# Image 0 of a deformable convolution: its rows moved in near and far rows by 18 transfers, and its gather indices made in three parts

## The chip, the cores and the metric

The kernel runs on one core of a Trainium2 chip. The metric is the device time in microseconds (us); lower is better. Before the change it is 1011.0 us, the median of 3 runs (1010.9 to 1011.95).

## The reference, cut to what matters

Four layers run one after the other on `x` of shape (2, 32, 64, 64), each on a group-normalised copy of `x` and added to it: an anchor-based normalisation, a graph-like feed-forward layer, a state-space scan over the 4096 pixels of an image, and a deformable 3x3 convolution. The change lies in the last one:

```
offset = _conv(data_im, offset_w)                    # 18 channels: y and x of 9 taps
mask = jax.nn.sigmoid(_conv(data_im, mask_w))        # 9 channels
col = _deform_im2col(data_im, offset, mask)          # bilinear samples at tap + offset, times mask
out = jnp.einsum('op,bphw->bohw', weight, col)
```

For every output pixel and tap the offset convolution says where to sample; the sample is a weighted sum of four corner pixels, all 32 channels of which are read.

## The kernel before, in words

The two images go through the last two layers one behind the other, and they overlap: while the scan of image 1 runs on DVE, ACT and PE, image 0 is already sampled. POOL (GpSimd) fetches the corners. A table in DRAM (`corner_table_0`, `corner_table_1`) holds for every pixel its four corners times 32 channels; one indirect DMA (L780) fetches, for 128 pixels and one tap, 128 rows of it. 128 pixels are a group: group g of an image holds 32 pixels in each of the four quarters of the image, and a quarter is 16 image rows, so that two groups are one image row in each quarter. An image has 32 groups, image 0 with 9 gathers each, image 1 with 6 (the other taps are computed densely). Five slots hold gathered groups. POOL waits at the head of its list for the whole table (`table_in`, L1578) and for the first indices (`idx_ready`, L1579), and before each group for a free slot (`prod_done`, L777); then it issues gather after gather.

`prepare(b)` makes what POOL needs for image b. For image 0 it runs between the scan of image 0 and the projection of image 1. Its steps, engine by engine, in the order in which each engine has them written down:

- DVE: statistics and normalisation (`g4`, L1306), transposition into the table (`tab`, L1311), copies of the right and lower neighbours (L1315 to L1321; L1321 takes what ACT has evicted), then a wait for the image rows (L1326), two memsets of the border columns (L1327, L1328), and after each half of the offset convolution `positions` and `corners` (L1337 to L1348), which write 16 groups of indices; behind them the coefficients, and then the projection of image 1.
- PE: the four shifts for the lower neighbours (L1265), and then, after `g3_ready`, the offset convolution (L1274) in two halves of 512 columns for each of 4 quarters and 3 kernel rows. The trace shows two PE instructions for each matmul of the code.
- ACT: issues three of the six image-row transfers (`load_image`, L1239), and behind them evicts the four shifts (L1288).
- SP (SyncE): issues the other three, then the table in two halves (L1251), each after the copies that it needs, and after the convolution the residuals (L1256).

`G3` holds the normalised image three times, shifted by -1, 0 and +1 pixels, on 96 partitions; `load_image` fills it by DMA from SBUF to SBUF, one transfer for each shift j and each half h of the image, 256 KB each:

```
first = W + h * HALF - (j - 1)
engine.dma_start(G3[32 * j:32 * j + 32, first:first + HALF],
                 g4[64 * b + 32 * h:64 * b + 32 * h + 32, :]).then_inc(l3["g3_in"], 16)
```

Of the kernel before, what the change touches and what calls it, by code (L numbers as in the profile page):

```python
# [20 lines left out]
B, C, H, W = 2, 32, 64, 64  # L21
# [69 lines left out]
def build(nc, x, mats, vecs, wts, bic, anchors, base, sel, out):  # L91
    ctx = ExitStack()
    with ctx:
# [613 lines left out]
        gathered = [sem(f"gathered{k}") for k in range(SLOTS)]  # L707

# [510 lines left out]

        def prepare(b):  # L1220
# [15 lines left out]
            def load_image(engine, h):  # L1236
                for j in range(3):
                    first = W + h * HALF - (j - 1)
                    engine.dma_start(G3[32 * j:32 * j + 32, first:first + HALF],  # L1239
                                     g4[64 * b + 32 * h:64 * b + 32 * h + 32, :]).then_inc(l3["g3_in"], 16)  # L1240

            def sync(sp):
# [3 lines left out]
                load_image(sp, 0)  # L1246
# [6 lines left out]
                sp.wait_ge(l3["off_psum"], 2 * b + 2)  # L1253
# [6 lines left out]
            def tensor(pe, between=nothing):  # L1260
# [8 lines left out]
                pe.wait_ge(l3["g3_ready"], b + 1)  # L1269
                for n in range(2):  # L1270
                    for q in range(4):
                        for dy in range(3):
                            first = q * QUARTER + n * BANK + dy * W
                            last = nc.tensor.matmul(PS[32 * q:32 * q + 32, 4 + n, :], wt[0:96, W_OFF + 32 * dy:W_OFF + 32 * dy + 32],  # L1274
                                                    G3[:, first:first + BANK], start=(dy == 0), stop=(dy == 2))
# [4 lines left out]
            def scalar(act, between=nothing):  # L1280
# [4 lines left out]
                load_image(act, 1)  # L1285
# [10 lines left out]
            def vector(v, between=nothing):  # L1296
# [29 lines left out]
                v.wait_ge(l3["g3_in"], 96 * (b + 1))  # L1326
                vchain(v, nc.vector.memset(cols[0:32, :, 0], 0.0))  # L1327
                tell(v, nc.vector.memset(cols[64:96, :, W - 1], 0.0), l3["g3_ready"], b + 1)  # L1328
# [5 lines left out]
                def positions(half):  # L1334
                    part = slice(16 * half, 16 * half + 16)
                    v.wait_ge(l3["off_psum"], 2 * b + half + 1)
                    vchain(v, nc.vector.transpose(om[:, part, :].rearrange("p g k -> p (g k)"), PS[:, 4 + half, :]))  # L1337
                    vchain(v, nc.vector.tensor_tensor(yx[:, part, :], om[:, part, 0:18], bases[:, part, :], ALU.add))

                def corners(half):  # L1340
                    part = slice(16 * half, 16 * half + 16)
# [6 lines left out]
                    nc.vector.memset(prime[:, 12 + 2 * b + half:13 + 2 * b + half], 0.0).then_inc(l3["idx_ready"], 1)  # L1348

                positions(0)  # L1350
                corners(0)
# [495 lines left out]
```

## Time and profile before

| | |
|---|---|
| median of 3 runs | 1011.0 us |
| the profiled execution's own time | 1014.24 us |
| its span | 1012.0 us |
| mean granted TensorE clock | 0.832 |
| busy: PE, DVE, POOL, ACT | 782.5, 837.1, 580.1, 387.0 us |
| image rows of image 0 issued | from 346.8 us |
| first gather of image 0 | 368.24 us |

Times in the rows are microseconds from the start of the span, durations in microseconds unless ns is said. PE is the matmul engine, PEld its weight load, DVE the VectorE, SPq and ACTq the sequencers of SP and ACT when they issue a DMA. A row of the timeline gives start, duration, engine, line, operation, output<-input, how many are merged in it, and in brackets the idle time before it with what ended it.

### The profile page before, as it was taken

To read this page: it belongs to the slowest core of one execution; us is meant where nothing else is said; L and a number is where in the kernel's file an instruction comes from. 1 tells how busy PE (TensorE), PEld (TensorE's weight loads), DVE (VectorE), ACT (ScalarE), POOL (GpSimd) and SP (SyncE) were. 2 spreads that over 40 slices of the span, in tenths; PEclk is the share of its full clock that TensorE was granted. 3 is DMA by queue.
4 is the path that set the end of the run, shared out by engine and by line. 5 is a ranking of instruction groups with operands and counts; after the bars stand their busy time and mean duration, and the time that the engine had idled before them with its cause. 6 is when DMAs were issued, how large, how long until landed. Compare 5 with 4: busy or idle time off the path is not lost.

```text
span 1012.0 us, 8286 instructions
## 1 busy us (share of the span) xinstructions
PE 782.5 (77%) x2365; PEld 377.3 (37%) x2365; DVE 837.1 (83%) x1161; ACT 387.0 (38%) x544; POOL 580.1 (57%) x528
## 2 busy tenths in 40 slices
PE   2345875677787688676788787869379999999997
PEld 1132322222222124534454444423264444444443
DVE  3889842789999858879998899985989998979884
ACT  1120046854454136311212121101049586776650
POOL 0000000076765037877777777777777777777774
PEclk9666987979999889567777677776559999999998
DMA  5000017000000361111111111128353745444422
GB/s 122 0 0 1 0 31 155 17 0 1 1 1 0 64 133 49 37 52 53 51 50 52 52 49 53 51 64 195 110 139 90 195 136 143 122 123 130 120 65 53
DMA packets 32339, 69.82 MB, mean 69 GB/s; under 512 B 12368, under 2 KB 12624, under 8 KB 31184
## 3 DMA queue, kind: packets, MB, share of 16 engines
q1 hardware_dynamic: 16080, 35.27, 13.2%
q0 software_dynamic: 15360, 31.49, 12.1%
q10 hardware_dynamic: 864, 2.64, 1.2%
q8 instruction: 16, 0.26, 0.1%
q14 instruction: 19, 0.16, 0.0%
HBM read 54.94 MB, written 5.77 MB: 60 GB/s over the span
## 4 chain that ended last, share of the span: by engine, by line
PE 42%; DVE 26%; POOL 7%; issue 6%; ACT 2%; DMA 1%; DVEq 0%; ACTq 0%; POOLq 0%
PE PS L1481 19%; POOL got L780 7%; DVE scratch L1174 6%; PE PS L815 5%; DVE scratch L1100 4%; DVE scratch L1181 3%; PE PS L1057 2%; PE PS L1042 2%; PE PS L1498 2%; DVE prodg L791 2%; PE PS L855 2%; DVE PS L1097 2%; PE PS L1274 2%; DVE prodg L795 1%; PE PS L914 1%
## 5 line engine op out<-in xcount | busy, mean ns | idle before, releaser
L780 POOL DMA_INDIRECT got<-corner_table,idx_slot x405 | 402.8, 995 | 123.4 <-issue 123.4
L1042 PE MATMUL PS<-parts,selb 96*128 96x512 bf16 (+1 forms) x256 | 88.4, 446 | 85.0 <-DVE scratch L1100 45.3
L1057 PE MATMUL PS<-scratch,wt 128*128 128x512 f32 x256 | 146.1, 701 | 0.5 <-DVE scratch L1181 0.5
L1481 PE MATMUL PS<-scratch,UZ 128*128 128x512 f32 (+1 forms) x288 | 133.6, 613 | 2.9 <-DVE scratch L1466 2.9
L780 POOL DMA_INDIRECT got<-corner_table,idx_all x75 | 84.9, 1132 | 60.6 <-DVE prime L1348 38.0
L821 ACT ACTIVATE G<-PS 128x32 f32 (+1 forms) x32 | 6.3, 197 | 250.7 <-PE PS L815 250.6
L815 PE MATMUL PS<-ln_g,w 128*128 128x32 f32 x576 | 101.9, 344 | 0.0
L815 PEld LDWEIGHTS PS<-ln_g,w 128*128 128x128 f32 x576 | 99.3, 268 | 0.0
L1564 POOL MEMSET w<- 128x1152 f32 x1 | 1.1, 1058 | 159.7 <-POOLq L599 159.7
L1042 PEld LDWEIGHTS PS<-parts,selb 96*128 96x128 bf16 x256 | 22.9, 116 | 158.2 <-DVE scratch L1100 59.1
L1458 ACT ACTIVATE scratch<-UZ,knot 128x512 f32<-128x512 f32 (+1 forms) x128 | 81.6, 708 | 0.4
L1481 PEld LDWEIGHTS PS<-scratch,UZ 128*128 128x128 f32 (+1 forms) x288 | 53.2, 193 | 74.9 <-issue 55.8
L1057 PEld LDWEIGHTS PS<-scratch,wt 128*128 128x128 f32 x256 | 58.5, 229 | 57.4 <-issue 47.9
L1100 DVE TENSOR_TENSOR_SCAN scratch<-scratch,carry,PS 128x1024 f32<-128x1024 f32 x32 | 75.1, 2347 | 1.1
L1150 POOL TENSOR_TENSOR scratch<-scratch 128x1024 f32<-128x1024 f32 x16 | 37.6, 2349 | 59.5 <-ACT scratch L1132 59.5
L1481 PE MATMUL PS<-XN,UZ 128*128 128x512 f32 x144 | 65.2, 601 | 0.0
L1139 ACT ACTIVATE PS<-XN,negA 128x1024 f32<-128x1024 f32 x32 | 35.8, 1118 | 60.8 <-DVE scratch L1174 60.8
L1466 DVE SCALAR_TENSOR_TENSOR scratch<-scratch,UZ 128x512 f32<-128x512 f32 (+1 forms) x72 | 45.4, 691 | 4.8 <-ACT UZ L1455 4.5
L1150 POOL TENSOR_TENSOR got<-scratch 128x1024 f32<-128x1024 f32 x16 | 37.6, 2348 | 17.7 <-ACT scratch L1132 17.7
L1466 DVE SCALAR_TENSOR_TENSOR XN<-XN 128x512 f32<-128x512 f32 (+1 forms) x72 | 45.4, 692 | 0.7 <-ACT XN L1455 0.5
L1105 DVE TENSOR_TENSOR scratch<-scratch,PS 128x1024 f32<-128x1024 f32 x32 | 39.1, 1221 | 8.3 <-PE PS L1042 8.2
L1466 DVE SCALAR_TENSOR_TENSOR scratch<-scratch,XN 128x512 f32<-128x512 f32 (+1 forms) x72 | 45.2, 689 | 0.2
(350 smaller groups left out, 1354.8 us busy)
## 6 DMA issues: line engine op xcount, KB each, us to landing
UZ<-dense_rows SPq DMA_DIRECT2D x24, 512.0 KB, 4.1
got<-corner_table,idx_slot POOLq DMA_INDIRECT x405, 2.5
UZ<-dense_rows SPq DMA_DIRECT2D x96, 64.0 KB, 2.2
XN<-ln_g SPq DMA_DIRECT2D x6, 256.0 KB, 5.8
got<-corner_table,idx_all POOLq DMA_INDIRECT x75, 2.5
corner_table<-scratch SPq DMA_DIRECT2D x1, 1056.0 KB, 10.4
corner_table<-XN SPq DMA_DIRECT2D x1, 1056.0 KB, 10.4
X<-in_x SPq DMA_DIRECT2D x4, 256.0 KB
```

What stands on the lines that cost most here:

```text
L780: pool.indirect_dma_start(got[:, slot, tap, :, :].rearrange("p k c -> p (k c)"), None, tables[b], bass.IndirectOffsetOnAxis(ap=index[:, ta ...
L815: last = nc.tensor.matmul(group_psum(slot), w3[:, t, :], colgs[slot][:, t * C:t * C + C], start=False, stop=(t == n - 1))
L1042: last = nc.tensor.matmul(PS[:, first + n, :], selb[:, which, j, :], parts[:, bass.ds(i * CHUNK + n * BANK, BANK)], start=True, stop=True)
L1057: last = nc.tensor.matmul(PS[:, 4 + n, :], wt[:, W_SUM:W_SUM + P], dBC[:, j % 2, n * BANK:(n + 1) * BANK], start=False, stop=(j == PAIRS - 1))
L1100: tell(v, nc.vector.tensor_tensor_scan(hs, dA[:, j % 2, :], banks(0, 2), carry[:, j:j + 1], ALU.mult, ALU.add), sc["h_done"], s + 3)
L1105: nc.vector.tensor_tensor(dBC[:, j % 2, :], hs, banks(2, 2), ALU.mult).then_inc(sc["hc_done"], 1)
L1139: nc.scalar.activation(banks(6, 2), dl[:, c * CHUNK:(c + 1) * CHUNK], ACT.Exp, scale=negA[:, j:j + 1]).then_inc(sc["exp_done"], 1)
L1150: nc.gpsimd.tensor_tensor(dBu[j % 2], dus[c % 2], Bs[j % 2], ALU.mult).then_inc(sc["dbu_done"], 1)
L1174: tell(v, nc.vector.tensor_tensor_scan(hs, banks(6, 2), dBu[j % 2], carry[:, j:j + 1], ALU.mult, ALU.add), sc["h_done"], s + 3)
L1458: nc.scalar.activation(ramps[k][rows, j, :], loads[k][rows, 1, :], ACT.Relu, bias=knot[rows, j:j + 1]).then_inc(de["ramps"], 1)
L1466: nc.vector.scalar_tensor_tensor(ramps[k][rows, j, :], ramps[k][rows, j, :], 1.0, hats[k][rows, :], ALU.min, ALU.mult).then_inc(de["prods" ...
L1481: last = nc.tensor.matmul(PS[:, n % 4, :], steps[rows, j, :, :].rearrange("p b c -> p (b c)"), ramps[k][rows, j, :], start=(j == 0), stop= ...
```

## The change

For image 0 alone each queue moves its image half in near rows (rows 0 to 2 and row 15 of each 16-row quarter, three shifts each, six transfers) and then in far rows (rows 3 to 14, three transfers). Two quarters go in one transfer, as two pieces per partition. That makes 9 transfers on SP and 9 on ACT. Near rows have a semaphore of their own (`g3_near`). DVE clears the border columns of near rows by six memsets and signals `g3_ready`; later it clears those of the far rows by two. The offset convolution and the index arithmetic run in parts of 4, 12 and 16 groups; on DVE `corners(0)` and the far memsets stand before `positions(1)`. POOL waits for the first part's indices before group 0 and for the second's before group 4. Image 1 keeps its six transfers, its two memsets and its two halves.

```diff
+        NEAR_ROWS, FAR_ROWS = ((0, 3), (15, 16)), ((3, 15),)
+            PARTS = ((0, 4), (4, 16), (16, 32)) if b == 0 else ((0, 16), (16, 32))
+            parts_before = 3 * b
-            def load_image(engine, h):
-                for j in range(3):
-                    first = W + h * HALF - (j - 1)
-                    engine.dma_start(G3[32 * j:32 * j + 32, first:first + HALF],
-                                     g4[64 * b + 32 * h:64 * b + 32 * h + 32, :]).then_inc(l3["g3_in"], 16)
+            def load_image(engine, h, row_ranges=((0, HALF // W),)):
+                for first_row, last_row in row_ranges:
+                    for j in range(3):
+                        first = W + h * HALF - (j - 1)
+                        lo, hi = first_row * W, last_row * W
+                        if len(row_ranges) == 1 and last_row < HALF // W:
+                            lo, hi = lo + (j == 2), hi - (j == 0)
+                        n = HALF // 2 if last_row < HALF // W else HALF
+                        engine.dma_start(G3[32 * j:32 * j + 32, first:first + HALF].rearrange("p (q n) -> p q n", n=n)[:, :, lo:hi],
+                                         g4[64 * b + 32 * h:64 * b + 32 * h + 32, :].rearrange("p (q n) -> p q n", n=n)[:, :, lo:hi]
+                                         ).then_inc(l3["g3_in"] if last_row - first_row > 3 else g3_near, 16)
...
-                load_image(sp, 0)
+                if b == 0:
+                    load_image(sp, 0, NEAR_ROWS)
+                    load_image(sp, 0, FAR_ROWS)
+                else:
+                    load_image(sp, 0)
...
-                pe.wait_ge(l3["g3_ready"], b + 1)
-                for n in range(2):
+                for k, (lo, hi) in enumerate(PARTS):
+                    if k < 2:
+                        pe.wait_ge(l3["g3_ready"], 2 * b + min(k, 1 - b) + 1)
+                    n, lo, hi = lo // 16, 32 * (lo % 16), 32 * ((hi - 1) % 16 + 1)
...
-                load_image(act, 1)
+                if b == 0:
+                    load_image(act, 1, NEAR_ROWS)
+                    load_image(act, 1, FAR_ROWS)
+                else:
+                    load_image(act, 1)
...
+                if b == 0:
+                    edges = [cols[32 * j:32 * j + 32, 1:H + 1, x].rearrange("p (q r) -> p q r", r=16) for j, x in ((0, 0), (2, W - 1))]
+                    v.wait_ge(g3_near, 16 * 12)
+                    vchain(v, nc.vector.memset(cols[64:96, 0:1, W - 1], 0.0))
+                    vchain(v, nc.vector.memset(cols[0:32, H + 1:H + 2, 0], 0.0))
+                    vchain(v, nc.vector.memset(edges[0][:, :, 0:3], 0.0))
+                    vchain(v, nc.vector.memset(edges[0][:, :, 15:16], 0.0))
+                    vchain(v, nc.vector.memset(edges[1][:, :, 0:3], 0.0))
+                    tell(v, nc.vector.memset(edges[1][:, :, 15:16], 0.0), l3["g3_ready"], 1)
...
-                positions(0)
-                corners(0)
-                positions(1)
+                for k in range(len(PARTS)):
+                    if k:
+                        corners(k - 1)
+                    if b == 0 and k == 1:
+                        v.wait_ge(l3["g3_in"], 16 * 6)
+                        vchain(v, nc.vector.memset(edges[0][:, :, 3:15], 0.0))
+                        tell(v, nc.vector.memset(edges[1][:, :, 3:15], 0.0), l3["g3_ready"], 2)
+                    positions(k)
                 tell(v, nc.vector.tensor_copy(msk, om[:, :, 18:27]), l3["mask_in"], b + 1)
                 between(1)
-                corners(1)
+                corners(len(PARTS) - 1)
...
-                    pool.wait_ge(l3["idx_ready"], 2 * b + 1)
+                    pool.wait_ge(l3["idx_ready"], 3 * b + 1)
                     for G in range(first, first + SLOTS):
+                        if G == 4:
+                            pool.wait_ge(l3["idx_ready"], 2)
                         group_gather(pool, b, G, G % SLOTS, idx_all[:, G * TAPS:(G + 1) * TAPS])
```

## Rows read from the trace of the kernel before

**Rows 1.** The page, busy time of each engine (us, share of span, instructions).

```profile
PE 782.5 (77%) x2365; PEld 377.3 (37%) x2365; DVE 837.1 (83%) x1161; ACT 387.0 (38%) x544; POOL 580.1 (57%) x528
```

**Rows 2.** Waits of POOL from 369 us on: us in total, times, longest.

```profile
POOL got L780 <- issue: 146.0, 479, 0.3
POOL got L780 <- DVE prime L1348: 38.0, 1, 38.0
```

**Rows 3.** Timeline of POOL, the first gather and the last.

```profile
368.24 1.12 POOL L780 DMA_INDIRECT got<-corner_table,idx_all  x1 [38.04 <-DVE prime L1348]
...
1000.95 0.94 POOL L780 DMA_INDIRECT got<-corner_table,idx_slot  x1 [0.30 <-issue]
```

**Rows 4.** Timeline of DVE, the last group of image 1.

```profile
1003.47 0.95 DVE L838 TENSOR_TENSOR prodg<-got,coef 128x768 f32<-128x768 f32 x1
```

**Rows 5.** Timeline of DVE, where it waits for the gather of group 4.

```profile
436.10 0.17 DVE L788 COPY idx_slot<-idx_all 128x9 uint32 x1 [4.79 <-DMA got<-corner_table,idx_all]
```

**Rows 6.** Chain that ended last, 346 to 369: start, us, what.

```profile
348.61 7.71 DMA G<-XN
...
356.42 0.12 DVE G L1327
...
356.64 0.12 DVE G L1328
...
356.81 7.72 PE PS L1274 x28
...
364.66 0.73 DVE scratch L1337
...
367.31 0.07 DVE prime L1348
```

**Rows 7.** Line L778, POOL's wait before a group: ns min/median/max, first and last start.

```profile
L778 POOLq EVENT_SEMAPHORE  x64: 17/17/632, 366.8 to 977.8; - x64
```

**Rows 8.** Timeline of SP, 345 to 372.

```profile
353.08 3.76 SPq L1251 DMA_DIRECT2D corner_table<-scratch  x2
```

**Rows 9.** DMA issues of 345 to 367: count, KB each, us to landing.

```profile
corner_table<-scratch SPq DMA_DIRECT2D x1, 1056.0 KB, 10.4
```

**Rows 10.** Windows over the convolution: PE, PEld, DVE, ACT, POOL, clock, DMA share, GB/s.

```profile
356.80:361.50 4.70, 4.69 (x12) 1.10 (x14) 0.00 (x0) 0.07 (x1) 0.00 (x0) 0.50 1.06 220
361.50:368.10 6.60, 6.58 (x39) 1.89 (x34) 2.47 (x7) 0.00 (x0) 0.00 (x0) 1.00 0.60 125
```

**Rows 11.** Line L1274, image 0: ns min/median/max, first and last start.

```profile
L1274 PEld LDWEIGHTS PS<-G,wt x48: 106/110/177, 356.8 to 367.1; 96*32 96x32 f32 x48
L1274 PE MATMUL PS<-G,wt x48: 592/592/1062, 356.8 to 367.5; 96*32 96x512 f32 x48
```

**Rows 12.** Windows, columns as in rows 10: the image rows, then the table.

```profile
347.70:355.70 8.00, 7.08 (x8) 1.59 (x8) 6.07 (x11) 2.43 (x5) 0.00 (x0) 0.50 0.98 197
355.70:365.90 10.20, 9.09 (x42) 2.62 (x44) 1.99 (x5) 1.17 (x1) 0.00 (x0) 0.71 0.99 206
```

**Rows 13.** Line L1239, image 0: ns min/median/max of an issue.

```profile
L1239 SPq DMA_DIRECT2D G<-XN x3: 512/592/1560, 346.8 to 348.0; - x3
L1239 ACTq DMA_DIRECT2D G<-XN x3: 515/1206/2362, 346.8 to 348.6; - x3
```

**Rows 14.** Timeline of SP earlier in the kernel: start, us of all.

```profile
157.13 4.46 SPq L590 DMA_DIRECT2D XN<-ln_g  x6
162.24 13.69 SPq L584 DMA_DIRECT2D XN<-ln_g  x12
...
180.00 0.90 SPq L1542 DMA_DIRECT2D w<-in_wts  x2
```

**Rows 15.** Timeline of ACT, 346 to 356.

```profile
346.83 4.14 ACTq L1239 DMA_DIRECT2D G<-XN  x3
351.02 1.14 ACT L1288 ACTIVATE scratch<-PS 64x512 f32<-64x512 f32 x2 [6.02 <-issue]
```

**Rows 16.** Timeline of DVE, 350 to 368.

```profile
355.60 0.68 DVE L1321 COPY scratch<-PS 64x512 f32<-64x512 f32 x1 [1.02 <-ACT scratch L1288]
```

More of the change, by code:

```diff
@@ L1273, in tensor @@
                             first = q * QUARTER + n * BANK + dy * W
-                            last = nc.tensor.matmul(PS[32 * q:32 * q + 32, 4 + n, :], wt[0:96, W_OFF + 32 * dy:W_OFF + 32 * dy + 32],
-                                                    G3[:, first:first + BANK], start=(dy == 0), stop=(dy == 2))
+                            last = nc.tensor.matmul(PS[32 * q:32 * q + 32, 4 + n, lo:hi], wt[0:96, W_OFF + 32 * dy:W_OFF + 32 * dy + 32],
+                                                    G3[:, first + lo:first + hi], start=(dy == 0), stop=(dy == 2))
                     last.then_inc(l3["off_psum"], 1)
@@ L1325, in vector @@
                 cols = G3.rearrange("p (y x) -> p y x", x=W)
-                v.wait_ge(l3["g3_in"], 96 * (b + 1))
-                vchain(v, nc.vector.memset(cols[0:32, :, 0], 0.0))
-                tell(v, nc.vector.memset(cols[64:96, :, W - 1], 0.0), l3["g3_ready"], b + 1)
+                if b == 0:
[7 more added lines that the diff above has]
+                    tell(v, nc.vector.memset(edges[1][:, :, 15:16], 0.0), l3["g3_ready"], 1)
+                else:
+                    v.wait_ge(l3["g3_in"], 96 * 2)
+                    vchain(v, nc.vector.memset(cols[0:32, :, 0], 0.0))
+                    tell(v, nc.vector.memset(cols[64:96, :, W - 1], 0.0), l3["g3_ready"], 3)
                 between(0)
@@ L1332, in vector, with positions, corners @@
                 gs = slice(b * GROUPS, (b + 1) * GROUPS)
[L1334 to L1337, printed above, removed]
+                def positions(k):
+                    part, half = slice(*PARTS[k]), PARTS[k][0] // 16
+                    v.wait_ge(l3["off_psum"], parts_before + k + 1)
+                    vchain(v, nc.vector.transpose(om[:, part, :].rearrange("p g k -> p (g k)"),
+                                                  PS[:, 4 + half, 32 * (part.start % 16):32 * ((part.stop - 1) % 16 + 1)]))
                     vchain(v, nc.vector.tensor_tensor(yx[:, part, :], om[:, part, 0:18], bases[:, part, :], ALU.add))
-                def corners(half):
-                    part = slice(16 * half, 16 * half + 16)
+                def corners(k):
+                    part = slice(*PARTS[k])
                     vchain(v, nc.vector.tensor_scalar(corner0[:, part, :], yx[:, part, :], 0.5, 0.0, ALU.subtract, ALU.max))
```

5 lines of the change are left out of this document (3 added, 2 removed).

## The prediction

> **What bounds the kernel now.** I read the page first. Its list of engines names no clear owner: DVE is busy 83% of 1012.0 us, PE 77%, POOL 57% [rows 1]. So I went to what each waits for. POOL's gathers (L780) stand in the waits with two releasers only: one wait of 38.0 us for the index signal of L1348, and 479 gaps of at most 0.3 us that are called issue [rows 2]. The reader is to see from this that once POOL has begun it never waits again: the first of its 480 gathers starts at 368.24, the last at 1000.95, and between them lie only the instruction itself and 0.30 us of issue [rows 3]. DVE takes up the last group at 1003.47 [rows 4], 2.5 us behind that last gather, and the kernel ends some 8.5 us later. At the beginning of the stream too DVE is ahead of it: it waits 4.79 us for the gather of group 4 at 436.10 [rows 5]. So the start of POOL's stream sets the end, one for one, and everything depends on what releases that start.
>
> The chain of waits before it goes: image rows land (7.71 us from the issue), two memsets, the offset convolution on PE (7.72 us up to its first half), DVE's transposition and index arithmetic from 364.66, the signal at 367.31 to 367.38 [rows 6], and 0.86 us behind it the gather [rows 3]. But POOL has a second condition, which the chain doesn't show since it came a little earlier: the corner table. POOL's first group waits (L778) from 366.8, 632 ns long [rows 7]; that wait can only begin once the table's has passed. The second half of the table, issued in the last half us of SP's 3.76 from 353.08 (about 356.4) [rows 8], lands 10.4 us after its issue [rows 9], which is the same 366.8. The index signal is the late one by only 0.6 us.
>
> **The change, part by part.**
>
> *Indices of the first 4 groups sooner.* Here the chain gets shorter. The convolution of a part of 4 groups has 24 PE instructions of 128 columns in place of 512. At the lower of the two clock levels 12 instructions start in 4.7 us, at the higher the other 36 in 6.6 (the 39 counted there hold 3 that began before) [rows 10]: 0.39 and 0.18 us each. A quarter of the columns makes 24 x 0.39 / 4 = 2.3 us; if the weight loads (177 ns at the slowest, [rows 11]) can't overlap, 24 x 0.18 = 4.3. I take 3. DVE's index arithmetic from 364.66 to 367.37 took 2.7 us for 16 groups [rows 6]; for 4 groups between 0.7 and 2.7, I take 1.3. The indices are ready near 362.5, about 5 us sooner. All but 0.6 us of that is covered by the table: what is late next is the table's landing. The greatest gain is 0.6 us.
>
> *18 transfers for 6, in front of that table.* From 347.7 to 355.7 the 16 DMA engines are 0.98 busy at 197 GB/s with the 6 x 256 KB of image rows, and from 355.7 to 365.9 0.99 busy with the table [rows 12]. There is no gap between the two, so every us that the image rows take longer moves the table. The bytes stay the same: 6 x 256 KB at 197 GB/s are 8.0 us, of which the near rows (4 of 16) are 2.0 and the far rows 6.0. But now each queue has to issue 6 near transfers before its first far one. An issue from SBUF to SBUF takes about 0.51 to 0.59 us when nothing backs it up (minimum and median of SP, [rows 13]); small ones take 0.45 (0.90 for two), and six in a row at L590 4.46, 0.74 each [rows 14]. I take 0.6, since the nearest rows are L1239's own. The two queues issue side by side, so the far rows are issued from 346.8 + 6 x 0.6 = 350.4 and flow, 1.1 us after the issue as the first did (346.77 to 347.7 or a little later), from 351.5. Plus 6.0 is 357.5, against 355.7: the table moves by +1.8 us. With 0.45 an issue it is +0.9, with 0.74 +2.6; if the near bytes never let the engines starve, 0.
>
> *What is queued behind the issues.* ACT issues its 9 before the four evictions L1288, which began at 351.02 right behind its 4.14 us of issuing [rows 15]; DVE's copies L1321 stand behind those, and in DVE's order the near memsets behind the copies. So near rows that land early are of no use before the last copy is done, now 355.60 + 0.68 [rows 16]: the DMA wait that the split is to shorten was already hidden to within 0.1 us (the rows landed at 356.32, the first memset starts at 356.42 [rows 6]). ACT's third issue took 2.36 us because its queue was backed up [rows 13]; the third far one will be held the same way until ACT's first far transfer is done. With far transfers of 1.0 us that is 351.5 + 2.0 + 0.4 = 353.9. Four evictions of 0.59 and a copy of 0.68 end at 357.0, +0.7. SP issues the first table half after the second copy (353.08 now, near 355.9 then), still in time for 357.5 if its data flow 1.1 us later; a further us on ACT would be paid by the table.
>
> *Memsets and the longer convolution.* Six small memsets instead of two cost 4 x 0.22 = 0.9 us (start to start, 356.42 to 356.64 [rows 6]). PE starts the first part near 358, then stands until DVE has done the first corners and the far memsets (1.3 + 0.4 us). At the prices of now (12 of the 48 full instruction lengths at the low level's, of which the first part holds 6, and 36 at the high level's) the rest takes 6 x 0.39 + 36 x 0.18 = 8.9 us, and the last part ends near 358 + 3 + 1.7 + 8.9 = 371.6 against 368.07 (367.5 + 0.59, [rows 11]). DVE's coefficients and the projection behind them come 3.5 us later. That is covered: DVE waits 4.79 us there for the gather of group 4 [rows 5], and POOL being later itself adds to it.
>
> *The new wait for group 4* stands before the 37th gather, at about 416 us; its indices are there by 370. Such a wait has a median of 17 ns [rows 7].
>
> Sum: +1.8 (table) - 0.6 (the index wait that it takes over) = +1.2 us, bounds -0.6 and +2.0. The profiled execution took 1014.24 us (span 1012.0 and 2.2 around it), so 1015.4; it ran 3.2 above the median of the runs, 1011.0. Carried over to that median: 1012.2.
>
> The Trainium skill, "DMA: Bandwidth & Descriptors", section "Rules for kernel authors", speaks against the change: transfers under 64 KB are mostly overhead and should be joined into large ones, and the near ones have 48 and 16 KB. The page's section "Anatomy of one DMA" gives some 2.0 us fixed for one (on the GpSimd path). If those didn't overlap, six on a queue would be an estimated 12 us, and the sum about +10. The small transfers of [rows 14] disagree: issued every 0.45 us, they don't wait for one another; so I keep the sum.
>
> **The rivals.**
>
> 1. *On time (no change, -0.6).* The near data flow while the far ones are being issued, DMA never starves, POOL starts on the table at 366.8 + 0.86. For it: same bytes. Against: for 3.6 us the queues can only feed 2.0 us of data. 1010.4.
>
> 2. *Held queue (slower).* The near transfers are issued at the pace of a backed-up queue. For it: twelve of 256 KB took 13.69 us at L584 [rows 14], 1.14 each, and ACT's second and third here were held. Six near ones then take 6.8 us, far data flow from 354.7 and end at 360.7: table +5.0, end +4.4, 1015.4. It decides from an issue of 0.8 us on (+3.0 table, +2.4 end). Against: those were held by 256 KB each, these have 48 and 16.
>
> 3. *Cold convolution (slower).* The small first part and the pause keep PE on its low level (1.2 of 2.4 GHz), as the eight matmul instructions between 347.7 and 355.7 stayed at 0.50 though PE was busy 7.08 of 8.00 us [rows 12]. All 42 remaining instruction lengths at 0.39 are 16.4 us, the last part ends at 379, +11; less 4.79 and 1.2 of cover, 5.0 beyond the forecast: 1017. The Trainium skill, "TensorE: Matmul & The Clock Gate", Part 1, says the low level is the default and sustained activity lifts it; by that rule a pause speaks for this rival, and the rise at 361.5 here [rows 10] agrees with it.
>
> 4. *As named (faster).* POOL starts on its indices: 362.5 + 0.86 is 363.4, -4.9 us, 1006.1. It needs a table that lands 4.9 us sooner, and the DMA engines have no free time for that [rows 12].
>
> **How the numbers follow.** Forecast 0.55, on time 0.19, held 0.17, cold 0.05, as named 0.04. A measurement of this kernel tells 0.2%, 2.0 us, from no change (1009.0 to 1013.0). Faster: rival 4 and a little noise, 0.05. Slower: rivals 2 and 3 and 0.06 of the forecast's upper end (0.74 and more an issue), 0.28. Same: 0.67. The range goes from rival 1 less 0.6 of spread between runs (1009.8) to rival 2 less a little, 1014.8; it leaves out rival 4, the cold case and the worst of the held one.
>
> **What would show it.** Of the changed profile: the index signal of the first part between 361 and 364; POOL's first gather released by the table, at 369.4 (367.6 for rival 1, 372.6 for rival 2, 363.4 for rival 4); nine issues on ACT ending near 354 and L1288 behind them; DMA below 0.9 busy between 348 and 351.5; the last convolution part ending between 370 and 373, and still a wait for the gather of group 4 on DVE; 480 gathers without a wait. I'd be wrong if POOL's stream were broken, or if the end moved by another amount than the first gather.

## The result, and the profile after

Slower, by 0.7%. Beside the kernel before, the changed kernel took 1018.44 us (median of 4 runs, 1017.38 to 1021.04) against 1011.48: ratio 1.0068, 95% interval 1.0049 to 1.0086. On another chip, in more runs (e5 below), it was 1018.86 against 1013.30: 1.0043, 1.0022 to 1.0065. The forecast was 1012.2 us, with a range up to 1014.8. The profiled execution took 1021.04 us.

Line numbers after the change are 1 higher up to about L1013 (L780 is L781, L791 is L792, L898 is L899, L1012 is L1013), and 11 to 38 higher behind `load_image`.

The page after, busy time of each engine, against [rows 1]: POOL has 4.2 us more for the same 480 gathers, DVE 0.8.

```profile
PE 781.2 (77%) x2388; PEld 376.6 (37%) x2389; DVE 837.9 (82%) x1174; ACT 386.9 (38%) x544; POOL 584.3 (57%) x528
```

POOL's waits from 369 us on (total, times, longest; [rows 2]) and its first and last gather ([rows 3]). The releaser is now the table, as predicted, and the stream behind it is as unbroken as before. But the first gather is 1.56 us later and the last one 5.79: the prediction had named it a sign of being wrong if the end moved by another amount than the first gather. The profiled execution is 6.8 us longer. The 1.0 us that is left lies behind the last gather: DVE takes up the last group 0.3 us later after it, and PE's last 14 instructions take 0.7 us more (3.25 us for 2.56, at a mean granted clock of 0.50 for 0.61 around them).

```profile
POOL got L781 <- issue: 145.7, 478, 0.3
POOL got L781 <- DMA corner_table<-scratch: 39.6, 1, 39.6
...
```

```profile
369.80 1.12 POOL L781 DMA_INDIRECT got<-corner_table,idx_all  x1 [39.59 <-DMA corner_table<-scratch]
...
1006.74 0.94 POOL L781 DMA_INDIRECT got<-corner_table,idx_slot  x1 [0.30 <-issue]
```

The steps ahead of it, from the timelines of SP, ACT, PE and DVE and the DMA issues: nine issues on each queue (0.60 and 0.65 us each by their medians, the longest 1.49 on SP and 1.98 on ACT), the DMA engines 0.54 busy between 348.0 and 351.5 (1.02 before; below 0.9 was predicted), ACT's evictions from 354.40, the table's second half issued 1.2 us later and 1 us longer on its way ([rows 8, 9]), the convolution with its pause of 2.10 us, the last positions at 373.80 (368.11 before), and, as [rows 5], a wait for group 4.

```profile
346.80 6.69 SPq L1250 DMA_DIRECT2D G<-XN  x9
356.37 1.67 SPq L1267 DMA_DIRECT2D corner_table<-scratch  x2
```

```profile
346.86 7.50 ACTq L1250 DMA_DIRECT2D G<-XN  x9
354.40 2.04 ACT L1310 ACTIVATE scratch<-PS 64x512 f32<-64x512 f32 x4 [9.38 <-issue]
```

```profile
358.26 2.79 PE L1292 MATMUL PS<-G,wt 96*32 96x128 f32 x24 [3.29 <-DVE G L1356]
363.15 10.61 PE L1292 MATMUL PS<-G,wt 96*32 96x384 f32 x48 [2.10 <-DVE G L1389]
```

```profile
corner_table<-scratch SPq DMA_DIRECT2D x1, 1056.0 KB, 11.4
```

```profile
373.80 0.72 DVE L1369 STREAM_TRANSPOSE scratch<-PS 128x512 f32<-128x512 f32 x1 [1.53 <-PE PS L1292]
...
441.36 0.41 DVE L789 COPY idx_slot<-idx_all 128x9 uint32 x1 [5.15 <-DMA got<-corner_table,idx_all]
```

Where the other 4 us come from is seen when the start of each group's first gather is compared: group 0 is 1.56 us late, group 2 1.93, group 4 4.89 (416.62 before, 421.51 after). Here is that stretch, group 2 on DVE with the gathers beside it. Before, DVE finds group 2 not landed and idles 1.28 us; the gathers take 0.94 to 1.13 us:

```profile
405.13 1.20 DVE L1012 TENSOR_TENSOR parts<-scratch,parts 32x1024 bf16<-32x1024 f32 x1
...
406.24 0.94 POOL L780 DMA_INDIRECT got<-corner_table,idx_all  x1 [0.30 <-issue]
...
407.62 0.17 DVE L788 COPY idx_slot<-idx_all 128x9 uint32<-128x9 uint32 x1 [1.28 <-DMA got<-corner_table,idx_all]
407.70 1.35 DVE L791 TENSOR_TENSOR prodg<-got,coef 128x1152 f32<-128x1152 f32 x1
...
408.73 1.13 POOL L780 DMA_INDIRECT got<-corner_table,idx_all  x1 [0.30 <-issue]
```

After, DVE comes late, finds everything ready, and each operation starts 0.07 us before the one ahead of it ends. The gather that starts at 410.66 takes 3.51 us, and ends at 414.17, 0.82 us behind the end of L792:

```profile
409.66 1.22 DVE L1007 TENSOR_TENSOR scratch<-PS,parts 64x1024 f32<-64x1024 f32 x1
...
410.66 3.51 POOL L781 DMA_INDIRECT got<-corner_table,idx_all  x1 [0.30 <-issue]
410.80 1.20 DVE L1013 TENSOR_TENSOR parts<-scratch,parts 32x1024 bf16<-32x1024 f32 x1
...
411.94 0.15 DVE L789 COPY idx_slot<-idx_all 128x9 uint32<-128x9 uint32 x1
...
412.01 1.34 DVE L792 TENSOR_TENSOR prodg<-got,coef 128x1152 f32<-128x1152 f32 x1
...
413.38 0.76 DVE L796 TENSOR_TENSOR prodg<-prodg 128x576 f32<-128x576 f32 x1
```

The kernel before has a larger such place of its own, the four additions L898: there a gather takes 6.98 us and ends 0.82 us behind L791. That is shown under e13.

Theory H: the end follows POOL's start *and* what DVE takes from the gathers; DVE's lateness, not the table, makes most of the loss. Rival R is my prediction (lateness is covered, only the start counts); rival A says that any shift of the gathers against DVE's operations is amplified; P that the smaller parts cost it. A gather is called held while it runs longer than the 0.94 us that it takes alone, beside operations of DVE.

### The profile page after: what moved, and what is told of

Same layout as the page of the kernel before. It is cut to its first block, busy times and chain, and to the rows that moved or that the text cites. A ratio compares the mean times of both kernels' runs of the same rounds, so it can differ in the third digit from the quotient of the medians.

```text
span 1018.8 us, 8359 instructions
## 1 busy us (share of the span) xinstructions
PE 781.2 (77%) x2388; PEld 376.6 (37%) x2389; DVE 837.9 (82%) x1174; ACT 386.9 (38%) x544; POOL 584.3 (57%) x528
## 3 DMA queue, kind: packets, MB, share of 16 engines
HBM read 54.94 MB, written 5.77 MB: 60 GB/s over the span
## 4 chain that ended last, share of the span: by engine, by line
DVE 26%; POOL 22%; PE 19%; issue 11%; ACT 2%; DMA 2%; ACTq 1%; DVEq 0%; POOLq 0%; SPq 0%
POOL got L781 22%; DVE scratch L1175 6%; PE PS L816 5%; DVE scratch L1101 4%; DVE scratch L1182 3%; PE PS L1519 3%; PE PS L1058 3%; DVE prodg L792 2%; PE PS L1043 2%; DVE PS L1098 2%; DVE prodg L796 1%; PE PS L1292 1%; DMA corner_table<-scratch 1%; PE PS L915 1%; DVE ln_g L799 1%
## 5 line engine op out<-in xcount | busy, mean ns | idle before, releaser
L781 POOL DMA_INDIRECT got<-corner_table,idx_slot x405 | 403.8, 997 | 123.4 <-issue 123.1
L781 POOL DMA_INDIRECT got<-corner_table,idx_all x75 | 88.1, 1175 | 62.2 <-DMA corner_table<-scratch 39.6
L816 PE MATMUL PS<-ln_g,w 128*128 128x32 f32 x576 | 98.0, 336 | 0.0
L816 PEld LDWEIGHTS PS<-ln_g,w 128*128 128x128 f32 x576 | 95.3, 259 | 0.0
## 6 DMA issues: line engine op xcount, KB each, us to landing
corner_table<-scratch SPq DMA_DIRECT2D x1, 1056.0 KB, 11.4
```

The source lines that it names most:

```text
L781: pool.indirect_dma_start(got[:, slot, tap, :, :].rearrange("p k c -> p (k c)"), None, tables[b], bass.IndirectOffsetOnAxis(ap=index[:, ta ...
L816: last = nc.tensor.matmul(group_psum(slot), w3[:, t, :], colgs[slot][:, t * C:t * C + C], start=False, stop=(t == n - 1))
```

## The experiments

e1 to e16 were timed in 5 rounds beside the kernel before, whose runs there spread from 1009.8 to 1019.0 us; a ratio is the kernel's to it, as measured, and need not be the quotient of the two medians. The positions of profiles are counted from the end of L1306 (`g4`; 346.75 us in the profile before), since the work ahead of that varies by some 3 us between the profiles. The table gives the first gather, the first gather of group 5 and the last gather against the profile before (21.49, 87.95 and 654.20 us behind that point). A profile is of one execution, which may lie anywhere in its kernel's spread: e10's took 1016.55 us against a median of 1011.43, e9's 1014.76 against 1008.62, e12's 1009.24 against 1012.47. So the last column does not follow the medians. Some expectations name group 4; the table has group 5, which lies behind the long gather at the additions. Before, that gather is the first of group 4, but in e1, e2 and e6 it falls into group 3, and group 4 begins 6.03, 7.41 and 8.98 us late for that reason.

| kernel | median us (before) | ratio, 95% interval | first gather | group 5 | last |
|---|---|---|---|---|---|
| changed | 1018.44 (1011.48) | 1.0068 (1.0049-1.0086) | +1.54 | +4.86 | +5.77 |
| e1 parts only | 1014.55 (1013.76) | 1.0003 (0.9984-1.0022) | +0.85 | +0.18 | -0.38 |
| e2 late gathers | 1015.27 (1013.76) | 1.0008 (0.9994-1.0022) | +1.74 | +1.47 | +1.16 |
| e3 late VectorE | 1016.56 (1013.76) | 1.0014 (0.9998-1.0030) | -0.08 | +2.44 | +3.44 |
| e4 changed, gap | 1017.80 (1013.76) | 1.0037 (1.0020-1.0054) | +1.55 | +2.39 | +3.64 |
| e5 changed again | 1018.86 (1013.30) | 1.0043 (1.0022-1.0065) | +1.58 | +4.93 | +4.93 |
| e6 no pause | 1017.14 (1013.30) | 1.0037 (1.0022-1.0053) | +3.01 | +3.04 | +5.28 |
| e7 before, 1 filler | 1010.37 (1013.30) | 0.9968 (0.9954-0.9982) | -0.07 | -3.39 | -3.54 |
| e8 before, 2 fillers | 1010.28 (1013.30) | 0.9973 (0.9958-0.9987) | -0.01 | -6.26 | -5.19 |
| e9 two-input fillers | 1008.62 (1013.31) | 0.9944 (0.9924-0.9963) | +0.01 | -4.94 | -1.67 |
| e10 one-input fillers | 1011.43 (1013.31) | 0.9971 (0.9954-0.9988) | -0.07 | -6.33 | -0.25 |
| e11 changed, 2 fillers | 1015.26 (1013.31) | 1.0010 (0.9991-1.0029) | +1.55 | -1.30 | -0.01 |
| e12 parts, 2 fillers | 1012.47 (1013.31) | 0.9987 (0.9969-1.0006) | +0.90 | -4.88 | -4.52 |
| e13 waits at L898 | 1008.94 (1012.71) | 0.9969 (0.9950-0.9987) | +0.20 | -4.19 | -4.73 |
| e14 waits | 1009.50 (1012.71) | 0.9966 (0.9953-0.9980) | -0.08 | -6.09 | -1.77 |
| e15 changed, waits | 1011.38 (1012.71) | 0.9985 (0.9972-0.9997) | +1.54 | -4.13 | -0.88 |
| e16 parts, waits | 1010.71 (1012.71) | 0.9978 (0.9962-0.9994) | +0.85 | -4.78 | -2.58 |

### e1 to e4: which part of the change costs

In the cuts, `vchain` and `tell` are the kernel's helpers: the operation signals its end, and the engine waits for that before its next one. e1, the parts without the transfers (in `changed`, with part 0 to bank 6; ACT's transfers and DVE's memsets go back to those of before in the same way):

```diff
-                if b == 0:
-                    load_image(sp, 0, NEAR_ROWS)
-                    load_image(sp, 0, FAR_ROWS)
-                else:
-                    load_image(sp, 0)
+                load_image(sp, 0)
...
-                    if k < 2:
-                        pe.wait_ge(l3["g3_ready"], 2 * b + min(k, 1 - b) + 1)
+                    if k == 0:
+                        pe.wait_ge(l3["g3_ready"], b + 1)
```

> The parts without the transfers: image 0's rows move in by the six transfers of the kernel before and one signal releases the convolution, which runs in parts of 4, 12 and 16 groups without a pause (part 0 in PSUM bank 6, so that it and part 1 do not share a bank); the gathers wait for each part's indices. Theory H (the end follows POOL's start plus what VectorE's operations with two SBUF inputs take from the gathers): POOL's first gather starts when the table lands, about 367.6 us (before 368.24), VectorE is late by some 1 us only (12 more matmuls, no pause), the table is not behind 18 transfers; the end is 0.6 us earlier to 1 us later than before: 1010.9 to 1012.5 us. Rival P (the parts themselves, with their smaller matmuls, are what costs): +3 us or more, with the transfers as before. Rival R (the end follows the first gather alone): -0.6 us.

No difference that can be told, and group 5 within 0.2 us: P falls. The first gather did not gain the 0.6 us but lost 0.85: the table's data ended as before (19.4 us behind `g4`), but the last of its 16 signals came at 21.45, 1.6 us behind the other 15 (in the kernel before the last came at 20.01). The last section comes back to it.

e2, in `before`:

```diff
                     pool.wait_ge(l3["idx_ready"], 2 * b + 1)
+                    if b == 0:
+                        nc.gpsimd.memset(got_flat[:, 3984:5760], 0.0).then_inc(waited, 1)
+                        pool.wait_ge(waited, 1)
```

> The kernel before with a POOL memset of 1776 elements (about 1.56 us by the 1.8 us of 2048) between the waits and the first gather; VectorE, TensorE and the transfers are untouched. Theory H: the gathers start 1.6 us later and VectorE, which is on time, waits that much longer at groups 2 and 4, so nothing new is taken from the gathers: end +1.3 to +2.0 us (about 1013.1). Rival R: +1.6 as well. Rival A (any shift of the gathers against VectorE's operations is amplified, and the shift by the table is enough for the whole loss): +5 to +7 us, group 4's gathers +4.9.

The gathers began 1.74 us late, a little more than in the changed kernel, and group 5 is 1.47 late, not some 4.9; the medians are 1.5 apart, and the interval ends at +2.2. A late start costs itself and is not amplified: A falls.

e3, in `before`:

```diff
                 corners(0)
+                if b == 0:
+                    for _ in range(8):
+                        vchain(v, nc.vector.tensor_copy(PS[:, 1, :], PS[:, 0, :]))
                 positions(1)
```

> The kernel before with eight copies from PSUM to PSUM (128x512, about 0.7 us each, 5.6 us) on VectorE between the first half's indices and the second half's positions, so VectorE goes on about 5.6 us late (as 5.69 in the changed kernel) while table and first gather stay where they are (368.2). Theory H: VectorE no longer idles at group 2 (1.28 us before), its two-input operations of that time run back to back and hold the gathers; group 4's first gather +2.5 to +4 us, end +3 to +5.5 us (1014.5 to 1017). Rival R (my prediction: lateness is covered by the 4.79 us wait at group 4): group 4 within 0.3 us, end 0 to +0.9 us. Rival A: 0.

DVE is 4.94 us late at the first weighing, POOL starts as before, and group 5 is 2.44 us late, the last gather 3.44. The gather of 3.51 us is there again, in the same place of DVE's list (timeline of POOL in e3):

```profile
407.12 1.31 POOL L780 DMA_INDIRECT got<-corner_table,idx_all  x1 [0.30 <-issue]
408.73 3.51 POOL L780 DMA_INDIRECT got<-corner_table,idx_all  x1 [0.30 <-issue]
412.55 0.97 POOL L780 DMA_INDIRECT got<-corner_table,idx_all  x1 [0.30 <-issue]
```

By the interval (0.9998 to 1.0030) the time alone does not tell +2.8 us from nothing; the trace does. R falls by its own number (group 4 within 0.3 us: it is 2.43 late).

e4, in `changed`, ahead of group 2's weighing in image 1's projection:

```diff
             low(0), left(2), low(1)
+            if b == 1:
+                for _ in range(2):
+                    vchain(v, nc.vector.tensor_copy(PS[:, 5, :], PS[:, 4, :]))
             between(2)
```

> The changed kernel with two copies from PSUM to PSUM (128x512, about 1.4 us in all) on VectorE ahead of group 2's weighing: VectorE does 1.4 us more work, at the place where the kernel before idled 1.28 us. Theory H: the gather that took 3.51 us at 410.66 ends while the copies run, group 4's gathers are 1 to 2 us earlier than in the changed kernel, and the end is 0.5 to 3 us earlier than the changed kernel's 1018.4 although VectorE does more. Rivals R and A (no lock by VectorE's operations): not earlier, or up to 1.4 us later.

The gather of 3.51 us is gone and group 5 is 2.47 us earlier than in the changed kernel (+2.39 for +4.86) although DVE does 1.4 us more. That is the trace's answer; the time (1017.80, 1.0037) is not separated from the changed kernel's in e5 (1018.86, 1.0043). The timeline of POOL in e4, at that place:

```profile
407.56 1.31 POOL L781 DMA_INDIRECT got<-corner_table,idx_all  x1 [0.30 <-issue]
409.17 0.94 POOL L781 DMA_INDIRECT got<-corner_table,idx_all  x1 [0.30 <-issue]
410.42 0.95 POOL L781 DMA_INDIRECT got<-corner_table,idx_all  x1 [0.30 <-issue]
411.67 0.94 POOL L781 DMA_INDIRECT got<-corner_table,idx_all  x1 [0.30 <-issue]
412.92 1.32 POOL L781 DMA_INDIRECT got<-corner_table,idx_all  x1 [0.30 <-issue]
```

### e5 and e6: the size, and the pause

e5 is the changed kernel, unaltered.

> The changed kernel, unaltered, beside the kernel before on one chip in more runs, since the runs of the kernel before spread from 1009.8 to 1018.1 us in the first four experiments. If the loss is the sum of the later gathers (e2_late_gathers, +1.5 us by the medians) and the late VectorE (e3_late_vector, +2.8 us): +4 to +5 us, ratio about 1.0045. If the first comparison (+6.9 us) has the size: ratio 1.0068. Rival N (the first comparison was mostly scatter and my +1.2 us stands): ratio 1.001 to 1.002.

The middle case: +5.6 us by the medians, 1.0043; N falls (its 1.002 lies just below the interval). The first gather and group 5 repeat to 0.1 us.

e6, in `changed` (part 0 in bank 6, as e1):

```diff
                     tell(v, nc.vector.memset(edges[1][:, :, 15:16], 0.0), l3["g3_ready"], 1)
+                    v.wait_ge(l3["g3_in"], 16 * 6)
+                    vchain(v, nc.vector.memset(edges[0][:, :, 3:15], 0.0))
+                    tell(v, nc.vector.memset(edges[1][:, :, 3:15], 0.0), l3["g3_ready"], 2)
...
-                    if b == 0 and k == 1:
-                        v.wait_ge(l3["g3_in"], 16 * 6)
-                        vchain(v, nc.vector.memset(edges[0][:, :, 3:15], 0.0))
-                        tell(v, nc.vector.memset(edges[1][:, :, 3:15], 0.0), l3["g3_ready"], 2)
```

> The changed kernel without the pause in the convolution: part 0 goes to PSUM bank 6 and the far edges are zeroed right behind the near ones (the far rows had landed by 358.4 us), so that TensorE runs the three parts without a stop; transfers, table and first gather as in the changed kernel (369.8). VectorE should be at the last part's positions 2 to 3.5 us earlier than in the changed kernel (373.8), so some 2 to 3.5 us late instead of 5.7. Theory H (late VectorE costs): group 5's gathers 1 to 2.5 us earlier than in the changed kernel, counted from the end of g4's making, and an end 1 to 3 us earlier than it. Rivals R and A (only the start of the gathers counts): as the changed kernel, within 0.5 us.

The last positions are 2.4 us late instead of 5.7, as expected, and between the first gather (+3.01) and group 5 (+3.04) nothing more is lost. So DVE being 2.4 us late, beside gathers that are 3.0 late, costs nothing. The first gather itself was 1.5 us later than in the changed kernel: its last table half landed 12.8 us behind its issue instead of 11.4, again with the last signal 1.5 us behind the other 15. So the time gained only 1.7 us on e5, which the intervals don't separate.

### e7 to e12: is it the gaps?

e7 and e8, in `before` (one and two fillers):

```diff
                 for c in range(NCHUNK):
+                    vchain(v, nc.vector.tensor_copy(PS[:, 5, :], PS[:, 4, :]))
                     project_delta(v, 1, c)
...
                 broadcast(pe, 0, 0, 0, 0, (sc["b_used"], NCHUNK * PAIRS + 1))
+                pe.wait_ge(pr["delta_ready"], 8)
```

> The kernel before with one copy from PSUM to PSUM (128x512, about 0.7 us) on VectorE ahead of each of image 1's four delta additions (L898, two SBUF inputs, 4.6 us back to back), and TensorE's first use of that PSUM waiting for them: VectorE does 2.8 us more, out of its 4.8 us of waiting at group 4. Theory H: the gather that took 6.98 us there is over sooner and up to three more run in the gaps: group 5's gathers 1 to 3 us earlier than before, end -1 to -3 us. Rival R (a gather is not held by VectorE's additions, or a gap of 0.7 us is too short to let one through): 0 to +1 us.

> As e7_gap_deltas, with two copies (1.4 us) ahead of each addition, 5.6 us more of VectorE, a little over its 4.8 us of waiting. Theory H: one gather passes in each gap at the least, group 5's gathers 2.5 to 4.5 us earlier than before, end -1.5 to -4 us, less what VectorE's lateness of about 1 us takes later. Rival R: +1 to +3 us, since VectorE is late.

Both are faster than before, by 3 us, while DVE does 2.8 and 5.6 us more; group 5 gains more than the 3 and 4.5 us that I expected at most (3.39 and 6.26). The gather of 6.98 us has become four of 1.56 us in e7, and e8 has none over 1.32 there.

e9 and e10 are e8 with other fillers:

```diff
-                        vchain(v, nc.vector.tensor_copy(PS[:, 5, :], PS[:, 4, :]))
+                        vchain(v, nc.vector.tensor_tensor(chunk_buffer(1)[:, 0:512], chunk_buffer(1)[:, 0:512],
+                                                          chunk_buffer(1)[:, 512:1024], ALU.add))     # e9
+                        vchain(v, nc.vector.tensor_copy(chunk_buffer(1), chunk_buffer(2)))            # e10
```

> As e8_double_gap_deltas (1010.3 us, 3.0 less than before by the medians), same place and count, but the two fillers ahead of each delta addition add two SBUF tiles (128x512 f32, about 0.7 us each) instead of copying within PSUM. Theory H (an operation with two SBUF inputs holds the gathers, and the gain of e8 is the gaps): the fillers close the gaps, the gathers are held for some 10 to 12 us in a row, group 5's gathers +4 to +6 us against before instead of -6.3, end +2 to +6 us (1015 to 1019). Rival W (the gain of e8 came from VectorE's or TensorE's new timing, or from the wait that was added, not from free gaps): about 1010.3, as e8.

> As e8_double_gap_deltas with fillers that copy SBUF to SBUF (128x1024 f32, one input, some 0.65 us). If only operations with two SBUF inputs hold the gathers: as e8, 1009 to 1012 us, group 5's gathers 5 to 6.5 us earlier than before. If every operation of VectorE on SBUF alone does: as e9, group 5 later than before by 3 us or more.

e9 is where theory H fell in its first form. Fillers with two SBUF inputs, which were to close the gaps, let the gathers through: 1008.62 us, none over 1.10 us beside them. DVE and POOL in e9, from the end of L1012 on:

```profile
416.82 1.40 DVE L1030 TENSOR_TENSOR scratch<-scratch 128x512 f32<-128x512 f32 x2
418.26 1.23 DVE L898 TENSOR_TENSOR XN<-XN,scratch 128x1024 f32<-128x1024 f32 x1
419.40 1.41 DVE L1030 TENSOR_TENSOR scratch<-scratch 128x512 f32<-128x512 f32 x2
```

```profile
416.62 1.10 POOL L780 DMA_INDIRECT got<-corner_table,idx_all  x1 [0.30 <-issue]
418.02 1.02 POOL L780 DMA_INDIRECT got<-corner_table,idx_all  x1 [0.30 <-issue]
419.35 0.95 POOL L780 DMA_INDIRECT got<-corner_table,idx_all  x1 [0.30 <-issue]
```

It isn't free time that they need. The fillers wait for their own end (`vchain`), so the second and the addition behind it start some 0.03 us after the end of the one ahead (418.22 to 418.26), and the gather of 418.02 is over 0.82 us after 418.22. e10 doesn't tell kinds of fillers apart for the same reason.

Over all 18 traces (before, changed, e1 to e16) I took every boundary between two DVE operations that a gather of over 1.15 us was waiting at: with a gap of 0.03 us the gather ended 0.82 us (within 0.06) behind the boundary 644 times, and stayed held twice; where the two overlap by 0.07 to 0.09 us it ended so 65 times and stayed held 85 times. (Held here: it ended more than 1.0 us behind; boundaries at which it ended at other distances are left out.)

These 150 overlaps sort by operation. Between two `tensor_tensor` operations all 37 stayed held, where with a gap all 631 were let through; the other 48 that stayed held stand at the small index copy before or behind such an operation. Of the 65 let through, 43 lie between two `scalar_tensor_tensor` and 18 before a copy of 64x128, later in the kernel, 3 before a copy within PSUM, and 1 before an index copy. The limit of 1.15 us leaves out short holds; one of these, the first gather above, ended 0.83 us behind L1012 (416.89) although the first filler overlaps it by 0.07 us. So the rule has exceptions.

e11 and e12 are `changed` and e1 with the fillers of e8.

> The changed kernel with the fillers of e8 (two PSUM copies ahead of each delta addition). Theory H: its first loss, ahead of group 4 (the stall of 3.5 us at 410.7), stays, the stall of 7 us at the additions goes, and VectorE, already 5.65 us late and now 5.6 us more with 4.8 us of waiting to pay from, is late behind group 4: group 5 some 5 us earlier than in the changed kernel, end 2 to 5 us earlier than it, 1014 to 1017 us. Rival R2 (in the changed kernel VectorE has nothing left to wait, so the fillers cost what they bring): within 1 us of it.

> The candidate for the fastest: the parts of e1_parts_only (six transfers, no pause, indices of the first four groups early) with the fillers of e8. The parts can bring 0.6 us where POOL starts at the table instead of the indices, and e1 measured no difference; so 1009.3 to 1011 us, as e8 or up to 0.6 us less, 2.5 to 4 us less than before.

e11 is as H expected (3.6 us below e5; group 5 6.2 us earlier than it); R2 falls. e12 is not the fastest: 1012.47 us, where I expected 1009.3 to 1011, with an interval that includes no change (0.9969 to 1.0006).

### e13 to e16: a wait instead of time

Theory G: a gather is let through where DVE's operations don't overlap, however small the gap. Rival T: it needs DVE free for some tenths of a us. e13, in `before`; e14 to e16 have it too, and the same `tell` or `vchain` at `left`, `low` and the copy L788 outside the scan loop (e14 in `before`, e15 in `changed`, e16 in e1):

```diff
-            nc.vector.tensor_tensor(dl[:, cols], dl[:, cols], log_tmps[b][:, cols], ALU.add).then_inc(pr["delta_ready"], 1)
+            tell(v, nc.vector.tensor_tensor(dl[:, cols], dl[:, cols], log_tmps[b][:, cols], ALU.add), pr["delta_ready"], 4 * b + c + 1)
```

> The kernel before with one thing: each delta addition (L898) waits for its own end before VectorE's next instruction is given, which leaves about 0.03 us between two additions in place of an overlap of 0.07 us; no filler, VectorE 0.4 to 0.5 us more. Theory G (a gather is let through where VectorE's operations do not overlap, be the gap ever so small, and is held as long as they do): at most one addition per gather, group 5's gathers 4 to 6 us earlier than before, end 3 to 5.5 us less, 1008 to 1010.5 us. Rival T (a gather needs VectorE free of two-input operations for some tenths of a us): as before, 1013 to 1014 us.

Before, DVE and POOL at the additions:

```profile
416.82 4.61 DVE L898 TENSOR_TENSOR XN<-XN,scratch 128x1024 f32<-128x1024 f32 x4
421.37 0.15 DVE L788 COPY idx_slot<-idx_all 128x9 uint32<-128x9 uint32 x1
421.44 1.34 DVE L791 TENSOR_TENSOR prodg<-got,coef 128x1152 f32<-128x1152 f32 x1
```

```profile
416.62 6.98 POOL L780 DMA_INDIRECT got<-corner_table,idx_all  x1 [0.30 <-issue]
423.91 0.97 POOL L780 DMA_INDIRECT got<-corner_table,idx_all  x1 [0.30 <-issue]
```

The same in e13: the four additions take 4.98 us instead of 4.61, and five gathers run where one did. The first still takes 2.23, since L1012 and the first addition still overlap.

```profile
416.89 4.98 DVE L898 TENSOR_TENSOR XN<-XN,scratch 128x1024 f32<-128x1024 f32 x4
```

```profile
416.69 2.23 POOL L780 DMA_INDIRECT got<-corner_table,idx_all  x1 [0.30 <-issue]
419.22 0.94 POOL L780 DMA_INDIRECT got<-corner_table,idx_all  x1 [0.30 <-issue]
420.47 0.96 POOL L780 DMA_INDIRECT got<-corner_table,idx_all  x1 [0.30 <-issue]
421.74 0.96 POOL L780 DMA_INDIRECT got<-corner_table,idx_all  x1 [0.30 <-issue]
423.00 1.25 POOL L780 DMA_INDIRECT got<-corner_table,idx_all  x1 [0.30 <-issue]
```

3.8 us less by the medians (0.9969, 0.9950 to 0.9987), with no filler: G holds here, T falls. DVE's wait for group 4 is gone with it (timeline of DVE in e13; [rows 5] before):

```profile
431.89 0.17 DVE L788 COPY idx_slot<-idx_all 128x9 uint32 x1
```

> As e13_waits_at_deltas, and the same wait at the subtractions of image 1's projection (left and low) and at the copy of indices ahead of each weighing outside the scan loop. Theory G: the stalls of 2.3 us at 399 go as well; another 0.5 to 1.5 us less than e13, about 1007 to 1009.5 us. Rival T: as before, or up to 1 us more for the waits.

Group 5 another 1.9 us earlier, the time the same as e13's (1009.50 and 1008.94): the further gain that I expected isn't measured. DVE's waits from 400 to 440 us, before and in e14 (total, times, longest), show the same of its waits for gathers: none is left in e14.

```profile
DVE idx_slot L788 <- DMA got<-corner_table,idx_all: 6.1, 2, 4.8
DVE parts L1012 <- ACT parts L966: 1.4, 1, 1.4
```

```profile
DVE scratch L1008 <- ACT parts L963: 2.0, 1, 2.0
DVE parts L1014 <- ACT parts L968: 1.4, 1, 1.4
```

> The changed kernel with the waits of e14. Theory G with lateness as its cause (in the changed kernel VectorE is 5.65 us late, finds its waits already met, and so its operations overlap and hold the gathers): with the waits the lateness costs the gathers nothing ahead of group 5; what is left of the change is its later table, +1.5 us, and what a late VectorE costs by itself: 1.5 to 3 us over e14, 1009 to 1012 us, 7 to 9 us less than the changed kernel (1018.9). Rival L (late VectorE costs otherwise, the overlaps only show it): 4 us or more over e14.

The changed kernel with waits is 1011.38 us, 7.5 below e5 (6.9 when each is set against its own runs of before), and 1.9 above e14, with intervals that overlap. Its group 5 is 1.96 us behind e14's, and of that 1.62 are there at the first gather. So with the overlaps gone the change costs its later table and little more; L falls.

> The parts without the transfers (e1_parts_only) with the waits of e14: the candidate for the fastest. POOL's first gather can start at the table, up to 0.6 us earlier than in e14, where the table's last signal does not come late; so e14 or up to 0.6 us less; if VectorE's later last part costs, up to 1 us more.

1010.71, 1.2 above e14 with intervals that overlap. The early indices could bring nothing: the table's last signal came as late as in e1 (21.45 us behind `g4`, e14 20.01), and the first gather 0.93 us later than in e14. e13 and e14 stand as versions that beat both kernels, by 0.3% (e9 too, by 0.6%, with idle work in it).

## Why the prediction was wrong, by its own steps

- *Issue price, table, ACT's order.* Right: 0.60 us an issue, ACT's evictions late as described (354.40), the table 2.2 us later (1.8 predicted), the index wait given back. The first gather came 369.80 (369.4 predicted), released by the table. Rivals 1, 2 and 4, with first gathers at 367.6, 372.6 and 363.4, are out; the 18 issues took 0.60 and 0.65 us by their medians, so the small ones did not wait for one another's landing.
- *Indices sooner.* Right: signal at 362.8 (362.5), and covered by the table.
- *Longer convolution.* Mis-sized: 5.7 us late at the last positions, not 3.5. The pause was 2.10 us (1.7), and the two later parts took 10.61 us (8.9). The granted clock was 0.50 (1.2 GHz) over the first part and 0.75 as a mean over the others, where the kernel before ran at 1.00 from 361.5 on [rows 10]. It rose to 1.00 at 368.4, about the middle of that stretch. That is rival 3 in small, and the small first part alone doesn't make it: in e1, with the same parts but no pause, the clock rose at 361.8 and the convolution took 11.32 us in all (11.26 before); in e6, without the pause but 1.5 us later at its start, it rose at 365.3 and the convolution took 12.26. With the pause of 2.10 us, in which PE stood, it took 15.50. The two windows (columns as in [rows 10]):

```profile
358.20:361.10 2.90, 2.79 (x24) 2.02 (x24) 0.01 (x1) 0.00 (x0) 0.00 (x0) 0.50 0.98 203
363.10:373.80 10.70, 10.61 (x48) 3.25 (x48) 2.12 (x7) 0.00 (x0) 3.08 (x4) 0.75 0.48 102
```

- *"That is covered: DVE waits 4.79 us there for the gather of group 4."* This is the step that failed. The wait at group 4 is no slack. It is the echo of a gather that DVE itself holds for 7 us: with that hold broken up the wait is gone (e13, e14). And before it, at group 2, the late DVE loses the short waits that kept its operations apart: they overlap and hold a gather 3.51 us. e3 has it with lateness alone, e4 undoes it with 1.4 us of gap, e15 with waits. So the gathers lost 3.3 us more between the first one (1.54 late) and group 5 (4.86), which the prediction put at nothing.
- *"The start of POOL's stream sets the end, one for one."* Half right. A stream without waits can still change its length: gather durations were in the trace (0.94 at the least, 6.98 at the most) and I took them as fixed. e2 shows something near the one for one where DVE is on time: 1.74 us at the first gather, 1.47 at group 5, 1.16 at the last.

The Trainium skill, "SBUF — State Buffer", section "Who interferes with whom", has what I missed: a DVE instruction with two SBUF inputs contends with a GpSimd instruction that reads SBUF, and the order of issue decides which of them blocks. The traces agree (a gather ends 0.82 us behind the end of such an operation) and go further: over operations that overlap it is mostly blocked for the whole chain, 6.98 us over the additions and L791. The section also reports that `tensor_tensor` was not seen to stall a DMA; the gathers here, which take their indices from SBUF, were stalled. That it is a port that is contended for no run here shows; the runs show when a gather ends.

Left open: why the overlaps of some operations let a gather through (65 of 150 did); how much of a gain at group 5 reaches the end (of e10's 6.3 us the profile, which is of its longest run, keeps 0.3, of e13's 4.2 all); and why the kernel before spreads over 9 us.

## What to carry to other kernels

A wait on an engine off the critical path is slack only if you know what makes it; look whether that engine causes it itself. When an instruction stream without waits bounds a kernel, list its longest instances and what runs beside them: their durations are not constants. Where DVE works on SBUF tiles beside POOL's gathers, a wait for its own end after each operation (0.1 us) can be worth several us; here the four in e13 brought 3.8.

## What was not expected of the hardware

- A gap of 0.03 us between two DVE operations lets a held gather through (644 of 646 boundaries); it then ends 0.82 us later.
- In the profiles of e1, e6, e12 and e16, and in no other of the 18, the last of the 16 signals of the table's second half came 1.5 to 1.7 us behind the other 15, though the data had landed on time, and the first gather followed it by 0.9 us. These four are the kernels whose convolution runs in parts without a pause, so it seems to go with the program and not with chance. In all four the packet of that signal ends 0.01 us behind a packet of 16 KB of instructions that took 0.88 us. Such a packet stands near the end of the table in every profile; that in these four the two shared a DMA engine is likely from the times but not shown.
